# A second expert FFN of 64 experts, worked by pairs of interleaved experts, with its results stored in blocks and gathered per token

## The reference, cut to what matters

```python
router_logits = x @ gate_w                      # 1024 tokens x 64 experts
top_vals, top_idx = top_k(softmax(router_logits), 8)
rw = top_vals / sum(top_vals)                   # scattered to 1024 x 64
g, u = x @ w_gate[e], x @ w_up[e]               # 256 -> 96
h = silu(g) * u * rw[:, e]
out = sum_e h @ w_down[e]                       # 96 -> 256
x = x + tanh(g_ffn[1]) * out
```

## Time and profile before

| what | value |
|---|---|
| median of 3 runs (lowest, highest) | 409.8 us (408.25, 410.25) |
| span of the profiled execution | 409.7 us |
| PE busy | 289.1 us, 71% |
| DVE busy | 231.8 us, 57% |
| POOL busy | 212.3 us, 52% |
| ACT busy | 138.5 us, 34% |
| DMA, mean over the span | 240 GB/s |

### The profile page before, as it was taken

The page is one execution under the profiler, slowest core; times in us unless marked ns, Lnnn a source line. Parts: engine busy times, 40 slices in busy tenths (PEclk is TensorE's granted clock), DMA queues, the critical chain, the costliest instruction groups (busy, mean ns, idle before and its releaser), DMA issues.

```text
span 409.7 us, 7438 instructions
## 1 busy us (share of the span) xinstructions
PE 289.1 (71%) x2042; PEld 234.1 (57%) x2042; DVE 231.8 (57%) x1114; ACT 138.5 (34%) x393; POOL 212.3 (52%) x257
## 2 busy tenths in 40 slices
PE   5898168127810610899876778989899977871997
PEld 1345057126810510788765666878788855541886
DVE  0799999989397472355632433565655533331352
ACT  2263354315634420244432233444444432320000
POOL 2632013013358777777777777777777774540000
PEclk9999999657975555799999899999999999975899
DMA  4899997270016633999999999749999999726991
GB/s 134 306 341 300 302 322 226 80 228 3 1 48 224 232 128 131 316 330 324 324 331 311 338 326 318 234 136 297 301 326 300 305 289 267 214 58 251 346 299 62
DMA packets 72983, 98.39 MB, mean 240 GB/s; under 512 B 13007, under 2 KB 66144, under 8 KB 71920
## 3 DMA queue, kind: packets, MB, share of 16 engines
q1 hardware_dynamic: 63728, 79.03, 63.0%
q0 software_dynamic: 9216, 18.90, 14.5%
HBM read 62.23 MB, written 39.85 MB: 249 GB/s over the span
## 4 chain that ended last, share of the span: by engine, by line
PE 44%; DVE 22%; DMA 14%; POOL 9%; issue 5%; SPq 3%; ACT 3%; DVEq 0%; POOLq 0%; ACTq 0%
PE psum L756 16%; PE psum L765 10%; POOL expert_rows L514 8%; PE psum L812 7%; DVE work L1036 5%; DMA token_picks<-down_w,target 5%; DVE top L1032 5%; PE psum L745 4%; DMA gu_w<-expert_rows 3%; DMA sim<-expert_rows 3%; DVE xn L1154 2%; DVE stats L1007 2%; PE psum L576 2%; PE psum L570 2%; DMA sim<-token_picks 1%
## 5 line engine op out<-in xcount | busy, mean ns | idle before, releaser
L765 PE MATMUL psum<-proj_t,gu_w 96*96 96x256 f32 x254 | 77.5, 387 | 5.0 <-DVE gu_w L1247 5.0
L514 POOL DMA_INDIRECT expert_rows<-x_rows,place_at x64 | 62.5, 977 | 23.8 <-issue 22.9
L534 POOL DMA_INDIRECT token_picks<-down_w,target x64 | 58.7, 917 | 25.1 <-issue 14.4
L534 POOL DMA_INDIRECT token_picks<-adj,target x63 | 57.8, 917 | 22.5 <-issue 13.7
L967 ACT ACTIVATE gu_w<-psum 96x96 f32<-96x96 f32 x127 | 31.3, 246 | 108.2 <-PE psum L756 107.7
L1247 DVE TENSOR_TENSOR gu_w<-gu_w,psum 96x96 f32<-96x96 f32 x127 | 31.6, 249 | 56.8 <-ACT gu_w L967 56.0
L756 PE MATMUL psum<-gu_w,wgu 128*96 128x96 f32 x504 | 56.0, 256 | 7.7 <-DVE gu_w L1242 7.6
L756 PEld LDWEIGHTS psum<-gu_w,wgu 128*96 128x96 f32 x504 | 49.8, 170 | 9.6 <-DVE gu_w L1242 9.3
L1242 DVE COPY gu_w<-psum 128x192 f32<-128x192 f32 x127 | 43.7, 344 | 0.0
L745 PEld LDWEIGHTS psum<-ident,gu_w 96*128 96x128 f32 x160 | 22.0, 145 | 30.0 <-issue 12.3
L745 PE MATMUL psum<-ident,gu_w 96*128 96x96 f32 x160 | 27.7, 256 | 15.0 <-DMA gu_w<-expert_rows 14.4
(11 more groups left out here) (182 smaller groups left out, 448.2 us busy)
## 6 DMA issues: line engine op xcount, KB each, us to landing
expert_rows<-empty_rows SPq DMA_DIRECT2D x1, 15360.0 KB, 69.8
wgu<-in_L_ffn_w_gate_up SPq DMA_DIRECT2D x57, 192.0 KB
proj_t<-in_L_ffn_w_down SPq DMA_DIRECT2D x113, 96.0 KB
gu_w<-expert_rows SPq DMA_DIRECT2D x80, 120.0 KB
base<-in_L_ffn_w_gate_up SPq DMA_DIRECT2D x35, 192.0 KB
sim<-expert_rows SPq DMA_DIRECT2D x48, 120.0 KB, 2.0
pen<-in_L_ffn_w_gate_up SPq DMA_DIRECT2D x21, 192.0 KB
gu_w<-in_L_ffn_gate_up_proj SPq DMA_DIRECT2D x4, 512.0 KB, 8.1
```

Of the source, the lines that this page charges most:

```text
L514: pool.indirect_dma_start(rows_dram, bass.IndirectOffsetOnAxis(ap=place_at[:, t, k:k + 1], axis=0), x_rows[:, t, :], None).then_inc(placed ...
L534: pool.indirect_dma_start(picks_dram, bass.IndirectOffsetOnAxis(ap=target[0:SLOTS, n, i:i + 1], axis=0), y_slots[n][0:SLOTS, i, :], None, ...
L765: last = pe.matmul(psum[0:SLOTS, 4 + e % 2, i * D:(i + 1) * D], h1_t[:, e % 2, i * SLOTS:(i + 1) * SLOTS], wd[:, n, :], start=True, stop=True)
```

## The change

- **Pairs.** Experts 2q and 2q+1 share a region of twice the rows, their rows interleaved (row 2r + h). The host lays their weights side by side. A pair has one x load (192 KB, 2 KB for each of 96 partitions), two weight DMAs (384 and 192 KB) and one y store (192 KB, from SP). There are 64 pairs, 128 units.
- **Rings.** x: 8 pairs. Weights: 16 pairs, so the turn keeps 16 pairs and 48 pairs are loaded. y: 4 pairs. The first phase runs by falling pair, the second by rising pair.
- **Rows.** A row of `expert_rows` is 256 numbers. y goes in blocks to a new DRAM tensor `expert_y`, in the order of the rows, by plain stores. POOL gathers for each tile and pick the 128 rows of y (64 gathers), DVE adds each with its weight (`add_pick`). The first half's 32 gathers are issued in the second phase, and its 32 additions stand one in a unit from unit 88. The second half's gathers wait for the last pairs' stores. The final PE sum, the target copies and the diagonals are gone.
- **Clears.** 12.6 MB of `expert_rows` and 14.9 MB of `expert_y` are cleared, where 15.7 MB were.
- **Starts.** The first four pairs' x loads wait for 8, 16, 24 and 32 scatters; the loads in SP's list stand behind all 16 pairs' weights. The second half's 32 x scatters follow directly.
- **The loop for overflow** has buffers of its own and stands at unit 72. Its list, the router weights and the picks' weights and rows are made by DVE in small steps, one to a unit.

```diff
-    UNITS = NR - 1
-    units = [(NE + e, e) for e in range(NE)] + [(e, e) for e in range(NE - 1, 0, -1)]
+    PAIRS = PHASES * NP
+    UNITS = 2 * PAIRS
-            sp.dma_start(by_expert[:, 0:CAP * ROW]...
+            sp.dma_start(by_pair[:, 0:2 * CAP * D]...
+            later_y = y_dram[Y_MAIN:].rearrange("(e p h) d -> p e (h d)", p=CAP, h=2)
+            sp.dma_start(later_y, empty_rows[0:CAP]...).then_inc(y_cleared, 16)
+            def load_rows(p):
+                n = p % X_RING
+                if p < TOP_K_EXPERTS // 2:
+                    sp.wait_ge(placed_a[p], 16 * 2 * HT)
+                if p >= X_RING:
+                    sp.wait_ge(xt_filled, 2 * (p - X_RING) + 2)
+                sp.dma_start(x_slots[n]..., rows_dram[pair_row(p):pair_row(p) + 2 * CAP]...)
+            def store_y(p):
+                n = p % Y_RING
+                sp.wait_ge(y_ready, 2 * p + 2)
+                sp.dma_start(y_dram[y_row(p):y_row(p) + 2 * CAP]..., y_slots[n]...).then_inc(y_landed[n], 16)
+            for p in range(PAIRS):
+                if p == OVER_AFTER - 1:
+                    total_over = run_over()
+                if p + X_RING < PAIRS:
+                    load_rows(p + X_RING)
+                if p + W_RING < PAIRS:
+                    load_weights(p + W_RING)
+                store_y(p)
-            def scatter(e):
-                pool.wait_ge(y_ready, e + 1)
-                    pool.indirect_dma_start(picks_dram, ...target[0:SLOTS, n, i:i + 1]...)
+            def gather(n):
+                t, k = pick_of(n)
+                if n >= G_RING:
+                    pool.wait_ge(summed, n - G_RING + 1)
+                pool.indirect_dma_start(gathered[:, n % G_RING], None, y_dram, ...gather_at[:, t, k:k + 1]...)
+            y_stored(NP - 1)
+            total_over = load_over(pool)
+            pool.wait_ge(over_landed, total_over * 16 + 1)
+            pool.wait_ge(gather_at_ready, 1)
+            for n in range(PICKS // 2):
+                gather(n)
+            for n in range(PICKS // 2, PICKS):
+                if n % (2 * HT) == 0:
+                    y_stored(PAIRS - 4 + (n - PICKS // 2) // (2 * HT))
+                gather(n)
+            def copy_y(u):
+                if h == 0 and p >= Y_RING:
+                    act.wait_ge(y_landed[p % Y_RING], 16 * (p // Y_RING))
+            def add_pick(n):
+                dve.wait_ge(gather_landed[n % G_RING], 16 * (n // G_RING + 1))
+                dve.scalar_tensor_tensor(out=x3[:, t], in0=gathered[:, n % G_RING], scalar=pick_w[:, t, k:k + 1], in1=x3[:, t], ...)
+            for u in range(UNITS):
+                if u == 2 * OVER_AFTER:
+                    run_over()
+                up_times_silu1(u)
+                if u + 2 < UNITS:
+                    copy_slots_t(u + 2)
+                if LIST_FROM <= u < WEIGHTS_FROM:
+                    list_over(u - LIST_FROM)
+                elif WEIGHTS_FROM <= u < FIND_FROM:
+                    router_weights(...)
+                elif FIND_FROM <= u < ROWS_FROM:
+                    find_picks(...)
+                elif ROWS_FROM <= u < ROWS_FROM + 7:
+                    find_y_rows(u - ROWS_FROM)
+                if SUM_FROM <= u < SUM_FROM + PICKS // 2:
+                    add_pick(u - SUM_FROM)
```

More of the change, by code:

```diff
@@ L201, in gated_layers_kernel, with flat @@
[L201 to L205, removed]
+        def flat(home):
+            return home[:].rearrange("p t s -> p (t s)")
@@ L387, in load_rows @@
[L387 to L391, removed]
-            emptied(sp, F_SCORE[B - 1])
-            for u in range(W_OWN):
-                load_weights(u)
-            sp.wait_ge(ebias_ready, NT)
-            for u in range(W_OWN, W_RING):
-                load_weights(u)
@@ L538, in _ @@
[L538 to L551 removed]
+            place_first_half(13, HT * TOP_K_EXPERTS)
@@ L749, in gate_up1, with transpose_slots @@
-            def gate_up1(e):
-                n = units[e][1] % W_RING
-                pe.wait_ge(xt_copied, e + 1)
-                pe.wait_ge(w_landed[n], w_count[e])
-                need(pe, h_ready, e - 1)
+            def transpose_slots(u):
+                p, h = u // 2, u % 2
+                if h == 0:
+                    pe.wait_ge(x_landed[p % X_RING], 16 * (p // X_RING + 1))
+                need(pe, xt_copied, u - 1)
+                for k in range(KC):
+                    last = pe.transpose(psum[:, h, k * CAP:(k + 1) * CAP], x_slots[p % X_RING][:, h, k * P:(k + 1) * P],
+                                        ident[0:CAP, 0:CAP])
+                last.then_inc(xt_filled, 1)
@@ L758, in gate_up1, with down1 @@
                 last.then_inc(gu_filled, 1)
-            def down1(e):
-                n = units[e][1] % W_RING
-                pe.wait_ge(h_ready, e + 1)
-                need(pe, y_ready, e - 1)
-                for i in range(SUBS):
-                    last = pe.matmul(psum[0:SLOTS, 4 + e % 2, i * D:(i + 1) * D], h1_t[:, e % 2, i * SLOTS:(i + 1) * SLOTS], wd[:, n, :],
-                                     start=True, stop=True)
-                last.then_inc(y_filled, 1)
+            def down1(u):
+                p, h = u // 2, u % 2
+                pe.wait_ge(h_ready, u + 1)
+                need(pe, y_ready, u - 1)
+                pe.matmul(psum[0:CAP, 4 + h, 0:D], h1_t[:, h], wd[w_slot(p)][:, h], start=True, stop=True).then_inc(y_filled, 1)
@@ L990, in _ @@
+            for u in range(UNITS):
+                if u == 2 * OVER_AFTER:
+                    run_over()
+                silu_gate(u)
+                if u:
+                    copy_y(u - 1)
+            copy_y(UNITS - 1)
         @block.vector
@@ L1289 @@
+            for n in range(PICKS // 2, PICKS):
+                add_pick(n)
 _INS = ["x", "ctx_512", "mask_SxS2_bk1", "mask_BxS2_bf0", "g_xattn", "g_ffn", "L0_xattn_Wq", "L0_xattn_Wk",
```

724 lines of the change are left out of this document (381 added, 343 removed).

## The result

| | before | after |
|---|---|---|
| median, lowest and highest of 4 runs each (us) | 409.73 (408.25 to 410.25) | 422.37 (420.35 to 422.67) |
| span of the profiled execution | 409.7 | 420.9 (its own time: 422.67) |
| PE busy | 289.1 | 259.4, 62% |
| DVE busy | 231.8 | 248.4, 59% |
| POOL busy | 212.3 | 155.7, 37% |

The ratio is 1.030, with a 95% interval of 1.025 to 1.034: slower by 12.6 us. The forecast was 394.1 and its range ended at 412. PE works 30 us less and POOL 57 us less, and the program is longer; so the time has gone into waits. Five views show where.

What follows compares the result with a forecast made beforehand. DMA, then PE, was taken as the next bound. PE's start at 166.3 and the units reach 324.4; clock and list 1.5, loop 5.4, DMA 8.7 + 6 give 346.0; landings, gathers, addition and store give 394.1, range 384 to 403.

Steps and rivals of the forecast that it cites:

- The start: Before the units: clears land at 130, SP free at 124, weights to 163, x at 165, PE begins at 166.
- The units' transfers: DMA in the units at 335 GB/s: 8.7 us lost in pairs 0 to 15 and 6 in pairs 36 to 51.
- The first stretch: Pairs 0 to 15: transfers need 54.7 us against 41 on PE, less 5 in hand: 8.7 us lost.
- The second: Pairs 36 to 51: 49 us of transfers against 41, less 5, gives 3; taken as 6 for bunching after the loop.
- The overflow loop: Loop at unit 72 costs 5.4 us as before, between 3 and 8.
- DVE at nothing: DVE's copy, product and step in a unit make 1.28 us, just fitting, so no loss; bounds 0 and 8 us.
- The gathers: At the end, the last 32 gathers on POOL at 1.26 us each, like x scatters: 40.5 us.
- the rival with dear gathers: Gathers cost more than scatters: 405 us at 1.6 us each, 418 at 2.0; chance 0.12.
- The store at the end: After the last addition, the final store takes 2.2 us to the span's end.
- slower by the y ring: Pairs 0 to 15 and 36 to 51: y stores behind weights, four pairs deep; 423 us at 286 GB/s; chance 0.12.
- PE alone: PE alone bounds the units, DMA at 401 GB/s: 14.7 us go, start gains about 8, 371 us; chance 0.25.
- The other two rivals: Gathers dearer than scatters (405 to 418 us, chance 0.12); late first-half gathers stall DVE from unit 88 (434, chance 0.03).

Runs made afterwards that it cites:

- e1: Both clears written from 128 partitions instead of 96, same bytes, against the changed kernel: 407.75 us, ratio 0.996 to the kernel before.
- e2: 8 y slots instead of 4, nothing else, against the changed kernel: 412.13 us, ratio 1.005 to the kernel before.
- e3: Each pair's y store put ahead of the weight loads in SP's list, against the changed kernel: 422.33 us, ratio 1.031 to the kernel before.
- e10: y stores ahead of weight loads in SP's list, against the changed kernel with 128-partition clears and 8 y slots (396.45 us): 397.55 us.
- e6: Weight loads of pairs 16 to 31 and 48 to 63 left out, y ring still 4, against the changed kernel: 399.22 us, ratio 0.973.
- e7: Last four gathers taken from POOL and replaced by plain SP loads, against the changed kernel: 417.59 us, ratio 1.020 to the kernel before.

## Why the prediction was wrong, step by step

The sum was 394.1 against a span of 420.9: 26.8 us. (The profiled execution's own time is another 1.8 us above its span.) The steps that failed are the landing of the clears and of the first x load, the loss of the later pairs, and the store at the end.

- **The start, +10.7.** SP was free when predicted, but by two errors that cancel, and issued the weights in the predicted 39 us (38.4). Two steps failed. "By bytes the new ones land at 138, at 344 GB/s at 96. I take 130, because larger rows can only help": they landed at 138.5, at the bound, because 96 source partitions were the limit, not the size of rows. And the x load was taken to land 2 us after 163, but weights *issued* by 162 are not weights *landed*: it needed 13.6. Its 16 completions lie between 166.6 and 175.8, half of them by 168.2. For most of the pairs loaded before it the first and last completions are about 11 us apart, against at most 5 in e1. So the uneven end of the clear is probably carried through the weights into this x load; no run separates this from the mere number of bytes. The bound of +8 for this start was too small. That PE could begin at 145 with x early was right (146.3 in e1).
- **The units' transfers, 23.2 instead of 14.7.** The first stretch was predicted at 8.7 and measured 6.2 up to unit 32 and 3.5 in the 16 units after it, since the backlog does not end with the last weight load: 9.7, the mechanism and the size right. The second failed: 6 predicted, 13.5 measured; it is the term that was mis-sized. Its step was "49 us against 41, less 5: 3. ... I take 6". The same 16.5 MB at the measured 311 GB/s (mean of five stretches from 300 to 350) are 53.1 us, 12.1 over PE, and none of the 5 us of credit is there, probably because the backlog of this stretch begins before it: weights are issued again from 275.4, ahead of the loop, and the share is 0.97 in 290 to 300. Some 1.4 us of the 13.5 are a second price of such a wait. The granted clock, at its upper level in the units else, shows this in two stretches of the changed kernel:

```profile
280.00:290.00 10.00, 6.98 (x40) 5.58 (x39) 2.93 (x13) 2.09 (x7) 0.00 (x0) 0.70 0.62 188
340.00:350.00 10.00, 8.36 (x63) 7.38 (x63) 5.69 (x18) 3.58 (x14) 5.01 (x6) 0.83 0.94 307
```

  PE is busy 0.36 of the 2 us from 340 to 342, and then the clock is at its lower level (0.50) from 342.4 to 345.3: gate-up to gate-up takes 345.00 - 342.54 = 2.46 us there, and the next 1.53, instead of 1.28 each. The ring of four is worth 12.8 of the 23.2 (e2), the order in the list nothing (e3, e10).
- **The overflow loop**: 7.9 us between the products of units 71 and 72, so 6.6 for the loop; predicted 5.4. The loop leaves PE idle (0.36 us busy from 282 to 284), and the granted clock is 0.50 from 284.5 to 290.5. Unit 72's gate-up is in that stretch and takes 1.49 us instead of 0.84, about half of the 1.2 missing. The sum had the lower clock at the start only.
- **DVE at nothing** was right: 27.4 of 30 us busy at 1.28 us a unit.
- **The rest of the units, 2.7**: e6, without a stall, needs 43.2 for its first 32 units, of which the sum had 42.5, and 42.1 for units 72 to 104, where it had 41. That is 1.8, and 1.1 of it is the clock after the loop: from the product of unit 72 to that of 73 e6 needs 2.47 us instead of 1.28. The other 0.9 was not located.
- **The gathers** were right: 32 from 371.62 to 411.43, 39.8 us, predicted 40.5; the rival with dear gathers falls.
- **The store at the end, +4.5.** "store 2.2" came from the kernel before, whose POOL had ended long before; here the span ends with POOL's DRAIN, for which SP waits 4.6 us (e7). Its DRAIN is there too, 8.75 us long, but under PE's sum:

```profile
L87 POOLq DRAIN  x1: 8752/8752/8752, 369.6 to 369.6; - x1
```

Together 10.7 + 8.5 + 1.2 + 2.7, less 0.9 in gathers and landing, and 4.5: 26.7.

The rival "slower by the y ring" gave 423 us and had 0.12. Its place is confirmed by e2. That its number meets the measured 422.4 is luck: it had 13 for the start (10.7), 18 for the first pairs (9.7) and 13 for the later ones (13.5), and nothing for the end. Its reason, "y stores behind weights", is refuted as an order in a queue (e3) and holds as a share of the engines (e6). The mistake in weighing it was the rate: the lowest rows, 301 and 265, came from the stretches that were nearest in kind, full engines with x, y and weights. I took 335, between weights beside x scatters (344) and the mean of the units (321). The rival "PE alone" falls by the DMA share of 1.05 at 294 GB/s with PE at 8 of 10. The Trainium skill's figure of about 358 GB/s, which the prediction quotes for this rival, was no ceiling here: e1's clears ran at 401. The fit of 2.0 us and the bytes at 436 GB/s, which the prediction quotes from the Trainium skill's "DMA: Bandwidth & Descriptors", section "Anatomy of one DMA", is given there for DMAs that POOL issues, and three of a unit's four were SP's; no term rested on it. The other two rivals fall as well: the gathers cost what the scatters do, and DVE waits for no gather in the units (its 30 waits for them, 24.2 us, all come after 375 us).

## What to carry to other kernels

A ring's depth is to be reckoned in bytes in flight over the lowest full-share rate that the trace shows, not over a mean, and a load is late by all that was issued before it, though it was issued in time. Where work is moved to the end of the program, look what it had been hidden under: here a DRAIN that the kernel before also paid, unseen. And when a fix at the start returns half of what the trace promised, the next limit is already in the trace (here POOL's scatters); combine it with the fix for the other loss before judging either. And a wait of PE can cost more than its length, when its granted clock falls with it.

## What the hardware showed that was not expected

- The rate of a large store from SBUF depends on the number of source partitions: 195, 302 and 401 GB/s from 48, 96 and 128, with a share of the engines near 1 in all three, and with 96 partitions a long tail at a share of 0.41 to 0.68 (100 to 130 us). The x loads, y stores and down weights of this kernel also have 96 partitions. A down load of 192 KB takes 12 to 14 us to land in the changed kernel, the gate-up load of 384 KB from the same queue, with 128 partitions, 5.3 to 9.9. What 128 partitions would give them was not tried.
- POOL's DRAIN at the program's end finishes 8.9 to 9.3 us after the end of its last indirect DMA in the changed kernel and all ten edits of it, and the span ends 0.2 to 0.3 us later; in the kernel before 7.8 us (378.35 against 370.6).
- Large DMAs hold up the queue behind them: with the first clear ahead (12.6 MB) the next issue was taken after 46.56 us, and with the second (14.9 MB) ahead too, the one after it after another 60.70.
